# Four-layer cross-attention kernel: the context normed once in the experts' stage, the last attention's context keys made in the third stage and loaded back from DRAM

## What is computed

```python
x = x + tanh(g_xattn[0]) * attention_16_heads(LN(x), ctx)
x = x + tanh(g_ffn[0])   * experts_64_top8(LN(x))
x = x + tanh(g_xattn[1]) * mlstm_cell(LN(x), ctx)
x = x + tanh(g_ffn[1])   * mixture_of_depths(LN(x))
x = x + tanh(g_xattn[2]) * L2_attention(LN(x), ctx)     # layer_norm(ctx, cln_g, cln_b) @ Wkv inside
x = x + tanh(g_ffn[2])   * chosen_expert_ffn(LN(x))
x = x + tanh(g_xattn[3]) * L3_attention(ctx, LN(x), mask)
x = x + tanh(g_ffn[3])   * quantised_linear(LN(x))
```

```python
xn = layer_norm(ctx, g1, b1)           # 512 tokens of context
ln_lat = layer_norm(LN(x), g2, b2)     # 512 latents
q = ln_lat @ Wq
k, v = split(concat([xn, ln_lat]) @ Wkv)   # 1024 keys, 16 heads of 64
out = softmax(q k^T / 8 + mask) v @ Wout
```

## Time and profile before

| what | value |
|---|---|
| median of 3 runs | 2944.42 us |
| the profiled execution's own time | 2945.35 us |
| its span in the profile | 2943.6 us |
| TensorE busy | 2481.0 us, 84% of the span |
| VectorE busy | 1828.4 us, 62% |
| ScalarE busy | 1170.7 us, 40% |
| GpSimd busy | 755.3 us, 26% |
| mean granted TensorE clock | 0.92 of full speed |

### The profile page before, as it was taken

How to read it: one execution, slowest core, us unless ns; L and a number is a source line. 1 busy time by engine, 2 the same in 40 slices (tenths; PEclk the granted TensorE clock), 3 DMA queues, 4 the chain that set the end, 5 groups by cost and what they waited for, 6 DMA issues and landing times. The chain is left out here.

```text
span 2943.6 us, 35609 instructions
## 1 busy us (share of the span) xinstructions
PE 2481.0 (84%) x12608; PEld 1335.9 (45%) x12608; DVE 1828.4 (62%) x4072; ACT 1170.7 (40%) x2095; POOL 755.3 (26%) x462
## 2 busy tenths in 40 slices
PE   6888972865888699889899979989988989997996
PEld 2333331323555344545554635554454545463554
DVE  5667745246867474477767357748437875835774
ACT  1433430212323153265544146635325653514662
POOL 1002352520000042043323023414203432402441
PEclk8999985875878799999999999999999999999998
DMA  7411006974200200244320124430023442012442
GB/s 226 136 37 21 11 15 206 316 249 150 87 8 3 106 1 1 87 108 119 97 79 8 73 61 118 116 111 11 8 88 100 116 108 79 1 52 71 110 125 73
DMA packets 112959, 257.06 MB, mean 87 GB/s; under 512 B 36198, under 2 KB 56294, under 8 KB 106762
## 3 DMA queue, kind: packets, MB, share of 16 engines
q1 hardware_dynamic: 93978, 220.26, 24.8%
q10 hardware_dynamic: 12656, 25.97, 3.6%
q0 software_dynamic: 6144, 8.48, 1.0%
HBM read 119.81 MB, written 29.69 MB: 51 GB/s over the span
## 5 line engine op out<-in xcount | busy, mean ns | idle before, releaser
L858 POOL TENSOR_SCALAR pbuf<-pbuf,recip 128x1024 f32<-128x1024 f32 x128 | 364.5, 2848 | 946.0 <-DVE recip L762 946.0
L807 ACT ACTIVATE pbuf<-ps,least 128x1024 f32<-128x1024 f32 x256 | 284.3, 1113 | 295.3 <-DVE least L755 219.5
L755 DVE CUSTOM_DVE_ANT_0 ps<-ps,mask 128x1024 f32<-128x1024 f32 x256 | 307.9, 1244 | 140.2 <-PE ps L687 139.2
L584 POOL TENSOR_SCALAR pbuf<-pbuf,recip 128x512 f32<-128x512 f32 x128 | 200.2, 1576 | 459.7 <-DVE recip L505 459.7
L687 PE MATMUL ps<-kH,qT 64*128 64x512 f32 x1024 | 267.4, 642 | 49.8 <-ACT pbuf L807 47.0
L712 PE MATMUL ps<-work,vh 128*64 128x256 f32 x2048 | 251.9, 390 | 0.0
L555 ACT ACTIVATE pbuf<-ps,least 128x512 f32<-128x512 f32 x256 | 172.7, 686 | 155.6 <-DVE least L495 155.6
L769 DVE STREAM_TRANSPOSE pbuf<-pbuf 128x2048 f32<-128x2048 f32 (+1 forms) x128 | 226.3, 1768 | 0.0
L1554 ACT ACTIVATE early<-ps 128x1536 f32<-128x1536 f32 x86 | 123.9, 1441 | 200.9 <-PE ps L1369 191.7
L1632 DVE TENSOR_REDUCE mh<-ps 128x3 f32<-128x1536 f32 x86 | 150.0, 1744 | 63.8 <-PE ps L1358 61.2
L712 PEld LDWEIGHTS ps<-work,vh 128*64 128x64 f32 x2048 | 138.3, 138 | 95.2 <-issue 36.6
(11 more groups left out here) (371 smaller groups left out, 4054.7 us busy)
## 6 DMA issues: line engine op xcount, KB each, us to landing
work<-pbuf SPq DMA_DIRECT2D x784, 96.0 KB, 2.5
work<-pbuf ACTq DMA_DIRECT2D x240, 96.0 KB, 2.9
early<-in_L_wgu SPq DMA_DIRECT2D x22, 768.0 KB
expert_rows<-zero_rows SPq DMA_DIRECT2D x16, 1024.0 KB, 11.5
yg<-expert_rows SPq DMA_DIRECT2D x16, 1024.0 KB, 6.0
early<-in_L_wd SPq DMA_DIRECT2D x22, 384.0 KB
arena<-in_L_wo SPq DMA_DIRECT2D x8, 1024.0 KB, 8.8
arena<-in_L_wff SPq DMA_DIRECT2D x4, 2048.0 KB, 9.3
```

What stands on the lines that cost most here:

```text
L584: nc.gpsimd.tensor_scalar(x, x, recip[:, n % 8:n % 8 + 1], None, mult).then_inc(probs_ready[1], 1)
L755: nc.vector.tensor_tensor_reduce(out=x, in0=x, in1=mask, scale=1.0, scalar=FMAX, op0=add, op1=ALU.min, accum_out=least[:, n % 8:n % 8 + 1])\
L807: nc.scalar.activation(to, x, ACT.Exp, bias=least[:, n % 8:n % 8 + 1], scale=-1.0, accum_out=sums[:, n % 8:n % 8 + 1]).then_inc(taken, 1)
L858: nc.gpsimd.tensor_scalar(unit(n), unit(n), recip[:, n % 8:n % 8 + 1], None, mult).then_inc(pool_divided, 1)
```

## The change

It has three parts. (1) In the experts' stage SyncE loads the context of the four batches (512 KB each, after the weights of pairs 14 to 17, and waits for each), VectorE norms it (seven steps a batch, two after each pair from pair 12), and SyncE stores it to DRAM (`cn_d`). The fourth stage loads `cn_d` in place of the raw context and norms no more. (2) In the third stage a new generator on SyncE, TensorE and ScalarE loads `cn_d`, transposes it (two sets of four transposes a batch), scales it, and makes the 8 key products of each batch; ScalarE copies each in the order of the blocks, and SyncE stores it to `k_d` and loads the key weights of a later one. (3) The fourth stage's `keys(g + 1, 0)` and the first one of `firsts` are gone; SyncE loads 256 KB of keys per group, after the moves of a half group with odd h.

```diff
@@ attention_moved
         def score(p):
             if p % NT == 0:
                 all_kept(need[p // NT])
+                if p:
+                    pe.wait_ge(keys_in, 16 * (p // NT))
@@
-    def mover(sp):
+    def mover(sp, b):
+        load_keys(sp, b, 1, keys_in)
         for h in range(N // 2):
             move(sp, h, cross if h + 1 < N // 2 else cross + stay)
+            if h % 2 and h // 2 + 2 < groups:
+                load_keys(sp, b, h // 2 + 2, keys_in)
@@ experts, SyncE
                     load_pair(sp, a, places[n % WEIGHTS], n, came[n % WEIGHTS])
+                    b = n - WEIGHTS
+                    if b < B:
+                        sp.dma_start(cn_tiles[b], a["ctx"][b]).then_inc(cn_in, 16)
+                        sp.wait_ge(cn_in, 16 * (b + 1))
+                for b in range(B):
+                    sp.wait_ge(cn_ready, b + 1)
+                    sp.dma_start(cn_d[b], cn_tiles[b]).then_inc(cn_out, 16)
@@ experts, VectorE
+                    if n >= NORMED:
+                        next(context_steps, None)
+                        next(context_steps, None)
@@ layer1
+    KEYS_AT = (13, 42, 145, 183)
+    KEYS_EVERY = (4.8, 4.8, 3.8, 3.8)
+    KEYS_BANK = (7, 3, 3, 7)
@@ layer1, TensorE
                     def broadcast(h):
                         if h:
                             pe.wait_ge(L["d_ready"], since("d_ready", h))
+                        elif b == 1:
+                            pe.wait_ge(key_kept, KEY_JOBS)
+                        elif r:
+                            pe.wait_ge(key_kept, 2 * KEY_JOBS)
@@
+                        if t == 1:
+                            pe.wait_ge(key_kept, KEY_JOBS * (2, 2, 3, 4)[b])
@@
+                def context_keys():
+                    for b in range(B):
+                        yield KEYS_AT[b]
+                        pe.wait_ge(cn_in, 16 * (b + 1))
+                        if b:
+                            pe.wait_ge(other["d_ready"], H1 * (1, 1, 2, 2)[b])
+                        for c in range(DC):
+                            if c:
+                                yield KEYS_AT[b] + 1.5
+                                pe.wait_ge(key_kept, b * KEY_JOBS + c)
+                            for t in range(NT):
+                                last = nc.tensor.transpose(bank[:, t * P:(t + 1) * P], cn[:, t, c * P:(c + 1) * P], ident)
+                            last.then_inc(key_ready, 1)
+                        for g in range(HP):
+                            n = b * HP + g
+                            yield KEYS_AT[b] + 3 + KEYS_EVERY[b] * g
+                            pe.wait_ge(wk_in[n % WK], 16 * (n // WK + 1))
+                            pe.wait_ge(key_kept, b * KEY_JOBS + DC + g)
+                            for c in range(DC):
+                                last = nc.tensor.matmul(bank, wk3[n % WK][:, c, :], cnTs[u][:, c, :], start=c == 0, stop=c == DC - 1)
+                            last.then_inc(key_ready, 1)
@@ layer1, ScalarE (after each)
+                            nc.scalar.activation(cn_tiles[u][:, g % 2 * S:(g % 2 + 1) * S].rearrange("p (j c k) -> p j c k", j=4, c=4),
+                                                 bank.rearrange("p (c j k) -> p j c k", c=4, j=4), ACT.Copy).then_inc(key_kept, 1)
@@ layer1, SyncE (after each)
+                            sp.dma_start(k_d[b, g], cn_tiles[u][:, g % 2 * S:(g % 2 + 1) * S]).then_inc(key_out[g % 2], 16)
+                            wk_load(n + WK)
@@ layers2to3
+        def load_keys(eng, b, g, came):
+            eng.dma_start(kH[g % 2][:, :].rearrange("p (j x) -> p j x", j=4)[:, :, 0:P],
+                          k_d[b, g].rearrange("p (j x) -> p j x", j=4)).then_inc(came, 16)
@@
-            following = [(0, "", q_job(wqx, latT, g + 1)), (2, "", keys(g + 1, 0)), (4, "scores", keys(g + 1, 1))] if g + 1 < HP else []
+            following = [(0, "", q_job(wqx, latT, g + 1)), (4, "scores", keys(g + 1, 1))] if g + 1 < HP else []
@@
-        firsts = [(2, lambda bank: key_product(0, 0, bank), "keys", 0), (3, lambda bank: value_product(0, 0, bank), "values", 0),
+        firsts = [(3, lambda bank: value_product(0, 0, bank), "values", 0),
@@
-            sp.dma_start(ctxb[:, :, :], a["ctx"][b]).then_inc(ctx_in, 16)
+            sp.dma_start(ctxb[:, :, :], cn_d[b]).then_inc(ctx_in, 16)
@@
-        norm_steps = [n for n in range(0, 7 * 8) if n % 8 >= 5][-15:] + [56, 57, 58, 59, 60, 61, 62]
+        norm_steps = [n for n in range(0, 7 * 8) if n % 8 >= 5][-8:] + [56, 57, 58, 59, 60, 61, 62]
```

193 lines of the change are left out of this document (135 added, 58 removed).

## The result

The changed kernel takes 2976.64 us (median; 2971.84 to 2994.49) against 2948.8 for the kernel before on the same chip, a ratio of 1.0117 with a 95% interval of 1.0087 to 1.0146: **slower**, by more than the 0.5% that a measurement tells from no change (the two medians alone stand at 1.0094). The forecast was 2941 us, with 2910 to 2968 as its range.

| stage | before | after | difference | forecast |
|---|---|---|---|---|
| first | 503.7 | 499.9 | -3.8 | 0 |
| experts | 131.1 | 138.1 | +7.0 | +2 |
| third | 356.5 | 394.9 | +38.4 | +25 |
| fourth | 1949.3 | 1937.5 | -11.8 | -30.5 |
| of it: groups of the last attentions | 846.3 | 825.3 | -21.0 | -25 |

A forecast was written before the change was run, and what follows sets the result against it. In the last attention's groups, TensorE ends one half and SyncE-issued moves the other, with 0.9 us of slack. 2945.35 - 25 - 3 - 2.5 + 2 + 25 = 2941.85 profiled, 2941 us as median; range 2910 to 2968.

The forecast's parts named there:

- the 3 us for the loops' norm and the first product: Loops' background norm and the heads' first key product removed: gain 3 us, bounds 0 and 6.
- Groups of the last attention: Last attention: 28 removed products gain 0.9 us each, 25 us, because moves come due then; bounds 11 and 54.
- The rival in which TensorE binds: Last attention: each removed product is worth its full 1.92 us, kernel at 2912 us; chance 0.13.
- Experts: Experts' stage: added loads and stores delay the last weights, a stall of 2 us, bounds 0 and 8.
- Start of the fourth stage: Fourth stage's start: the context's norm goes, gain 2.5 us, between 0 and 5.5.
- the constants bound there: Sign at the fourth stage's start: starting no sooner after its barrier would show that VectorE's constants bind.
- Third stage: Third stage: added key work costs 25 us, lower bound 5, upper bound 47; stage at about 384 us.
- First pair: Third stage, first two batches: four keys of the first cost 4 us, four of the second 7; others and SyncE 0.
- Middle: Third stage, 901 to 931: two key products of the third batch and the fourth's transposes cost 4 us.
- End: Third stage's end: seven of the fourth batch's products, 1.75 us each less 1.9 us of gaps, cost 10 us.
- The slower rival: Third stage: key products hold up the mLSTM, cost 47 us, stage over 43 us longer, kernel 2963 us; chance 0.19.
- The clock rival: Third stage: added jobs raise TensorE's clock, so the stage costs only 8 us, kernel 2924 us; chance 0.17.

The follow-up runs named there:

- Run 14: Run 5's kernel with SyncE's last-attention key loads from the third group on left out; groups 827.9 us against 819.8, ratio 1.0056.
- run 13: Run 5's kernel with the latents' key product of each later group cut to half; groups 820.8 us against 819.8, ratio 1.0036.
- Run 4: The changed kernel with an unread key product put back in each last attention's head; ratio 1.0076, median 2969.54 us, heads 54.2 us.
- run 3: The changed kernel with the second batch's normed context loaded behind the first batch's first key store; ratio 1.0072, third stage 388.1 us.
- run 2: The changed kernel without SyncE's four waits for the raw context in the experts' stage; ratio 1.0121, that stage 134.4 us.
- run 10: Run 5's kernel with the second batch's keys placed behind that batch's first broadcast in all engines' orders; ratio 1.0007, third stage 382.7 us.
- run 11: Run 5's kernel with the third batch's context load and keys placed earlier; ratio 1.0062, third stage 393.3 us.
- runs 8 and 9: Run 5's kernel with each third-stage key product cut to half, then to one of eight parts; ratios 0.9998 and 0.9951, third stage 377.9 and 368.7 us.
- run 6: The kernel before with only the context's norm moved into the experts' stage, without SyncE's waits, keys made as before; ratio 1.0001.
- runs 11 and 12: Run 11, then its placement with run 10's and the first batch's keys closer together; ratios 1.0062 and 1.0031, third stage 393.3 and 388.9 us.
- run 5: The changed kernel with the edits of run 2, run 3 and Run 4 together; ratio 1.0048, median 2960.25 us, third stage 388.6 us.

## Why the forecast was wrong

The sum forecast 3.5 us off the profiled execution, and it got 29.8 longer. The 33.3 us between them are: third stage 13.4, heads 9.1, experts 5.0, groups 4.0, start of the fourth stage 1.7, the 3 us for the loops' norm and the first product, which gave nothing, with scatter 3.9; less the 3.8 of scatter in the first stage.

**Groups of the last attention: right.** "So the half shrinks from 13.96 to about 13.1 us, and the other one not at all". Measured -21.0 us for 28 groups, 0.75 each where the forecast had 0.9 (kernels without the product have 819.8 to 827.9 us, the kernel before 846.3 and 849.5); the exponents wait for moves in both halves. Run 14 shows that SyncE's loads cost nothing there, as forecast, and run 13 that less work on TensorE would buy no more. The rival in which TensorE binds is out.

**Head: the step that failed most clearly.** "The first of `firsts` go as well. TensorE's first product stands beside the norm of x, which ends as late." It does end as late, and yet the heads grew by 9.1 us. The term was put at a gain, and the price of what comes behind it was left out. Without the removed product TensorE stands 1.87 us ahead of the transposes, and the granted clock is at its lower level (0.50, 1.2 GHz) when the two products on the path come: 3.78 and 3.20 us for 1.98 and 1.88. With it, the slow stretch, where there is one, falls on products that nobody waits for yet. Run 4 gives all of it back with work that nobody reads, and in run 3 one head had the slow stretch early by itself and was as short as before. The Trainium skill's page "TensorE: Matmul & The Clock Gate", section "What's actually happening", says that the throttled state is the default and activity releases it. By that rule, which I applied to the stage that gets work, I should have asked the same of the place that loses work; the trace agrees, with 0.50 over the two products for 1.00 with the product in place (run 4).

**Experts: mis-sized.** Priced as "SyncE waits for each of the four loads with no other in its queue, 2.15 us each". There were pairs of weights ahead of each, and the waits were 16.8, 7.8, 7.9 and 8.0 us. These waits explain at most 2 of the 7 us, however (run 2). The rest comes with the moved norm, and by the estimate of run 2 with its bytes: I looked for free time at 616 to 635, where only the last weights' effect shows, and not at the share of 0.94 over the whole stage.

**Start of the fourth stage: 0.8 for 2.5.** The sign named in the forecast, "the constants bound there", is what the trace shows: VectorE's first copy waits for `wo2f`, 11.0 us behind the stage's start.

**Third stage: +38.4 for +25, the largest miss.** The loss at four marks, from the stage's start: 22.0 us at the first store of x, 23.8 at the second, 24.5 where batch 3's first mLSTM product runs, 38.4 at the end.
- First pair, forecast 11, measured 22 to 24. The failing steps are "Products planned at 45 to 59 [...] fall into the windows where VectorE is full: 0" and "Cost 0 there" for SyncE. VectorE was full, but the broadcast that it was to feed stands behind these keys in TensorE's order; run 10 moves them and gets 5.9 us. And the second batch's context load stood behind the first batch's last key: 6.8 us, run 3. With both mended the first store of x is 11.5 us later than before (181.5 for 170.0), near the 11 of the forecast. The lower level costs more than the 3.40 us that I took: 3.75 (run 11). I named the pattern ("what is queued behind it comes late too") and did not look at what is queued there.
- Middle, forecast 4, measured under 1.
- End, forecast 10, measured 14. Not seven but all eight products of the fourth batch stand in a full TensorE there, start to start 1.72 us each, 13.8 us: two ahead of batch 2's output tiles, four among and behind them, two in batch 3's hidden part. The kind was right; the count was one short. Two products of the third batch and the fourth's transposes stand behind this mark too, some 5 us; gaps and slower matmuls of the kernel before hide them, as far as the timelines tell. (The bound of 47 also counts 18 products where the sum's terms have 17.)

**The rivals.** The slower rival (key products hold up the mLSTM) named the right kind of loss; its own mark, over 43 us, was not reached. That its 2963 comes out near the result with the head's 9 and the experts' 5 us more is luck: its 47 for the third stage is 8.6 too much, and 4 us of groups and 5.6 of the other terms of the fourth stage are missing from it. The clock rival's mechanism also happened: the clock rose to 0.83 and the other matmuls gave back 27 us of busy time. But runs 8 and 9 show 0.7 us of stage for each us of product all the same.

**The balance.** The change buys 21 us with products that were worth 0.75 us each in their old place, and pays for them at a place where they cost 32 us with the load in time, 1.0 us each. With the mends of runs 3, 4 and 10 it is level (run 10; by stages of its profile: experts +5.3, third +26.2, fourth -26.4). The norm's move is level by itself (run 6).

**Open.** Why the third batch's early keys cost 5 us (runs 11 and 12) I only argued from the timeline. What the last 26 us in run 10 split into was not measured; runs 8 and 9 split the 32 us of run 5.

## What to carry to other kernels

Work moved off the busiest engine is worth what the next bound leaves, here 0.75 us of a product of 1.9, and it costs its full price wherever TensorE runs without a gap. Before moving work, price both places, and read the destination in each engine's own order: a load behind the last use of the previous tile, or a product ahead of a small matmul for which another engine waits, costs more than its length. And before removing a product beside someone else's wait, ask at which clock the next ones will run, and whether it was the one that took the slow stretch.

## What was not expected of the hardware

- Adding an unread product of four matmuls made each head 1.5 to 3.0 us shorter. In the first head, with 1.87 us of idle TensorE ahead of the transposes, the next two products ran at 3.78 and 3.20 us, with 0.16 us of idle at 1.98 and 1.88.
- It depends on little: the same head with the same code took 12.1 us in one profile, where the clock fell a product earlier and was back for the two on the path, and 15.1 in the three others.
- The reverse was small: fillers that raised the clock in the third stage's idle starts (with the keys, 35 us of pauses over 1 us in the place of 53; with the norm alone, 50 in the place of 82) shortened it by little: 3 us with the keys, and with the norm alone 0.6 to 2.3, which is no more than two profiles of the same code differ (353.4 and 355.1). That VectorE and transfers bound there is argued.
